# Gate weights, zeroing, denominators and expert stages moved in a fused attention and mixture-of-experts kernel

## What is computed

```
a   = attn(cond(x))             # cond: shared gated FFN and one of 3 typed gated FFNs, mixed by a gate
x   = x + a                     # attn: 16 heads of 16, causal, softmax, output projection
z   = cond2(x)                  # three shared FFNs and two of four typed ones, mixed by a gate
x   = x + ffn(z)                # router of three layers, top 2 of 8 experts, capacity 10 per sequence
```

## Time and profile before

| | |
|---|---|
| median of three runs | 2598.01 us (2594.25 to 2600.58) |
| the profiled execution | 2599.39 us, of which the span of the trace is 2597.7 us |
| PE busy | 2396.5 us, 92% of the span |
| PE weight loads | 1567.3 us, 60% |
| DVE busy | 1206.0 us, 46% |
| ACT busy | 1105.8 us, 43% |
| POOL busy | 124.6 us, 5% |
| chain that ended last | PE 79%, DVE 7%, ACT 6%, issue 3%, DMA 2% |

### The profile page before, as it was taken

One profiled execution on the slowest core, in us unless ns is written; L12 is line 12 of the kernel. 1 busy time (PEld: TensorE's weight loads), 2 busy tenths in 40 slices (PEclk: granted clock), 3 DMA queues, 4 the chain that ended last, 5 costly groups with the idle time before them and its releaser, 6 DMA issues.

```text
span 2597.7 us, 52267 instructions
## 1 busy us (share of the span) xinstructions
PE 2396.5 (92%) x18863; PEld 1567.3 (60%) x18880; DVE 1206.0 (46%) x2299; ACT 1105.8 (43%) x2097; POOL 124.6 (5%) x146
## 2 busy tenths in 40 slices
PE   6999999977988999999999999988999997689976
PEld 2444788876777444444448888883444443566654
DVE  5553455436987442333324333334443433955542
ACT  3553454434665432333323333323433342866650
POOL 0000000004331000000000000000000000000000
PEclk9999999988999999999999999998999999599995
DMA  3330111012332320210100000012111100042315
GB/s 114 98 101 29 42 49 49 16 41 61 87 99 58 100 101 25 73 57 26 56 33 25 33 12 12 12 45 65 33 32 48 48 1 1 0 146 90 98 41 129
DMA packets 145077, 141.94 MB, mean 55 GB/s; under 512 B 74608, under 2 KB 129904, under 8 KB 138416
## 3 DMA queue, kind: packets, MB, share of 16 engines
q1 hardware_dynamic: 128720, 84.01, 10.9%
q0 software_dynamic: 6864, 47.98, 5.4%
q10 hardware_dynamic: 9360, 8.13, 1.3%
HBM read 96.04 MB, written 39.85 MB: 52 GB/s over the span
## 4 chain that ended last, share of the span: by engine, by line
PE 79%; DVE 7%; ACT 6%; issue 3%; DMA 2%; SPq 1%; POOL 1%; ACTq 0%; DVEq 0%; POOLq 0%
PE ps L628 30%; PE ps L645 23%; PE ps L876 13%; PE ps L865 3%; PE ps L990 2%; PE ps L978 2%; PE ps L710 1%; DVE arena L1750 1%; PE ps L1024 1%; PE ps L742 1%; ACT misc L1276 1%; ACT arena L1275 1%; ACT misc L1153 1%; DMA arena<-eout_d 1%; ACT arena L1152 1%
## 5 line engine op out<-in xcount | busy, mean ns | idle before, releaser
L628 PE MATMUL ps<-xh,arena 128*128 (+1 forms) x5376 | 907.4, 312 | 18.3 <-DVE xh L1403 10.4
L645 PE MATMUL ps<-misc,arena 128*128 128x256 f16 (+1 forms) x4128 | 727.4, 313 | 9.2 <-DVE misc L1471 7.4
L628 PEld LDWEIGHTS ps<-xh,arena 128*128 (+1 forms) x5376 | 527.6, 98 | 288.8 <-issue 23.9
L645 PEld LDWEIGHTS ps<-misc,arena 128*128 (+1 forms) x4128 | 403.5, 98 | 223.0 <-issue 8.6
L1475 DVE SCALAR_TENSOR_TENSOR misc<-ps,misc 128x256 f16<-128x256 f32 (+1 forms) x480 | 254.9, 531 | 541.7 <-ACT misc L1085 540.8
L1085 ACT ACTIVATE misc<-ps 128x256 f16<-128x256 f32 (+1 forms) x480 | 225.0, 469 | 552.7 <-PE ps L628 552.7
L876 PE MATMUL ps<-arena 128*128 128x512 f16 x1536 | 332.8, 379 | 0.0
L876 PEld LDWEIGHTS ps<-arena 128*128 128x128 f16 x1536 | 149.7, 98 | 179.6
L1684 DVE TENSOR_TENSOR arena<-misc,arena 128x512 f16<-128x512 f32 x128 | 88.6, 692 | 254.8 <-ACT arena L1223 254.8
L1469 DVE TENSOR_TENSOR arena<-ps,misc 128x256 f32<-128x256 f32 (+1 forms) x208 | 105.2, 506 | 145.8 <-ACT misc L1081 144.7
L1222 ACT ACTIVATE misc<-ps,bias 128x512 f32<-128x512 f32 x128 | 87.8, 686 | 188.2 <-PE ps L876 181.2
(11 more groups left out here) (228 smaller groups left out, 2015.8 us busy)
## 6 DMA issues: line engine op xcount, KB each, us to landing
wstage<-in_m_w POOLq DMA_DIRECT2D x16, 1024.0 KB, 5.2
arena<-src_d SPq DMA_DIRECT2D x64, 256.0 KB, 3.8
src_d<-misc SPq DMA_DIRECT2D x24, 512.0 KB, 3.1
wstage<-in_c_wi POOLq DMA_DIRECT2D x6, 1024.0 KB, 5.7
wstage<-in_r_w POOLq DMA_DIRECT2D x5, 1024.0 KB, 5.4
eout_d<-misc SPq DMA_DIRECT2D x80, 64.0 KB, 1.9
arena<-eout_d ACTq DMA_DIRECT2D x4, 1280.0 KB, 17.5
cexp_d<-misc SPq DMA_DIRECT2D x18, 256.0 KB, 2.5
```

What stands on the lines that cost most here:

```text
L628: last = mm(ps[:, bank, col:col + p.n], weight(off, half, g, wp, k * F + f * 128), xh[:, xp, k, ds(start, p.n)], start=(k == 0 and n == 0) ...
L645: last = mm(ps[:, 4 + 2 * half + m, 0:p.n], weight(place[0], half, 2 if p.gated else 1, wp, f * D + m * 128), hid[:, st % 4, hp, 0:p.n], s ...
```

## The change

1. SP loads c_g0 and c_g1 between `stores(cs)` and `stores(ce)`; c_g1 gets columns of its own.
2. POOL no longer zeroes; DVE does, in front of `selectors`. SP's blocks of q no longer wait for POOL's zeroing, and `y_made` counts without it.
3. In PE's attention round the denominators stand between q's projection and k's. In DVE's, `o_f` stands in front of `x1_lo`.
4. PE's expert stages are fully written out, with the first layer three stages ahead and three PSUM banks; ACT reads the same banks.
5. The weight pieces move to stages 2, 3, 5, 6 (ACT) and 4 to 7 (DVE), all in the wide half. The scaling of eb2 moves from before the experts to behind stage 3 of the first.

```diff
-        gate_w2c = misc[:, 1024:1028].rearrange("p (k j) -> p k j", k=2)
+        gate_w2c = misc[:, 5632:5636].rearrange("p (k j) -> p k j", k=2)
...
         def y_made(c):
-            return 2 + 2 * (c + 1)
+            return 2 * (c + 1)
...
-            pool.wait_ge(ce.l2, 2 * ce.iters)
-            nc.gpsimd.memset(qbd_all.bitcast(F32), 0.0).then_inc(s["y_make"], 1)
-            nc.gpsimd.memset(vbd_all.bitcast(F32), 0.0).then_inc(s["y_make"], 1)
             pool.wait_ge(s["gates"], 1)
...
             stores(cs)
-            stores(ce)
-
             sp.wait_ge(s["x_lo"], 8)
             sp.dma_start(misc[:, 4608:5632], a["c_g0"]).then_inc(s["gw_in"], 16)
-            sp.dma_start(misc[:, 1024:1028], a["c_g1"]).then_inc(s["gw_in"], 16)
+            sp.dma_start(misc[:, 5632:5636], a["c_g1"]).then_inc(s["gw_in"], 16)
+            stores(ce)
...
                 sp.wait_ge(s["qk_lo"], c * 2 + 1)
-                sp.wait_ge(s["y_make"], 2)
...
-                if 0 <= i - 1 < NA:
-                    denominators(i - 1)
                 if ahead:
                     pe.wait_ge(s["y_lo"], i + 2)
                     if i - 2 >= 0:
                         pe.wait_ge(s["norm"], 2 * (i - 1))
                     projection(i + 1, 0)
+                if 0 <= i - 1 < NA:
+                    denominators(i - 1)
+                if ahead:
                     projection(i + 1, 1)
...
-                        last = mm(ps[:, st % 2, 0:n], w16(MOE_W[par][0], wp, k * F + f * 128),
-                                  xe[:, xp, k, ds(e * PER_E + c0, n)],
+                        last = mm(ps[:, (e * 16 + st) % 3, 0:n], w16(MOE_W[e % 2][0], wp, k * F + f * 128),
+                                  xe[:, xp, k, e * PER_E + c0:e * PER_E + c0 + n],
...
-            def expert(e, par, lastone=False):
-                for st in range(16):
-                    expert_out(e, par, st)
-                    if st + 2 < 16:
-                        expert_in(e, par, st + 2)
-                    elif not lastone:
-                        expert_in(e + 1, 1 - par, st - 14)
-            for st in range(2):
-                expert_in(0, 0, st)
-            expert(0, 0)
-            expert(1, 1)
-            with pe.Fori(1, NE // 2 - 1) as half_e:
-                e = half_e * 2
-                expert(e, 0)
-                expert(e + 1, 1)
-            expert(NE - 2, 0)
-            expert(NE - 1, 1, True)
+            for g in range(3):
+                expert_in(0, g)
+            for g in range(NE * 16):
+                expert_out(*divmod(g, 16))
+                if g + 3 < NE * 16:
+                    expert_in(*divmod(g + 3, 16))
...
-                    if st in (3, 4, 11, 12) and e + 1 < NE:
-                        expert_weight_high(e, int(st >= 11), int(st in (4, 12)))
+                    if st in (2, 3, 5, 6) and e + 1 < NE:
+                        expert_weight_high(e, int(st >= 5), int(st in (3, 6)))
...
+            v.memset(qbd_all, 0.0)
+            v.memset(vbd_all, 0.0)
             selectors()
...
                 if 0 <= i < NA:
                     probs_low(i, 0)
+                if 0 <= i - 1 < NA:
+                    dve.wait_ge(s["pv_mm"], 2 * i)
+                    dve.wait_ge(s["den_out"], i)
+                    v.tensor_tensor(o_f.rearrange("p k n -> p (k n)"), ps[:, 4, :], rden, ALU.mult).then_inc(s["norm"], 1)
                 if 0 <= i - 2 < NA:
                     dve.wait_ge(s["x1_hi"], i - 1)
                     cols = ds((i - 2) * CH, CH)
                     v.scalar_tensor_tensor(xh[:, 1, :, cols], x1, SX, xh[:, 0, :, cols],
                                            ALU.mult, ALU.subtract).then_inc(s["x1_lo"], 1)
-                if 0 <= i - 1 < NA:
-                    dve.wait_ge(s["pv_mm"], 2 * i)
-                    dve.wait_ge(s["den_out"], i)
-                    v.tensor_tensor(o_f.rearrange("p k n -> p (k n)"), ps[:, 4, :], rden, ALU.mult).then_inc(s["norm"], 1)
...
-            dve.wait_ge(s["eb2_in"], 16)
-            link(v.tensor_scalar(misc[:, 4608:6656], misc[:, 4608:6656], SEO, None, ALU.mult))
+            def bias_scaled():
+                dve.wait_ge(s["eb2_in"], 16)
+                link(v.tensor_scalar(misc[:, 4608:6656], misc[:, 4608:6656], SEO, None, ALU.mult))
...
+                    if fresh and st == 3:
+                        bias_scaled()
...
-                    if st in (5, 6, 12, 13) and not lastone:
-
-                        w, h = int(st >= 12), int(st in (6, 13))
+                    if st in (4, 5, 6, 7) and not lastone:
+
+                        w, h = divmod(st - 4, 2)
```

18 lines of the change are left out of this document (8 added, 10 removed).

## The result

| | before | after |
|---|---|---|
| median of five executions | 2598.01 us | 2573.07 us |
| lowest to highest | 2594.25 to 2602.52 | 2569.20 to 2587.09 |
| profiled execution, its span | 2599.39, 2597.7 | 2570.97, 2569.1 |

The change makes the kernel 0.9911 of what it was, interval 0.9896 to 0.9927: 24.9 us by the medians, where 37.5 were forecast. The forecast was 2560.5 in a range of 2551 to 2573; the median of 2573.07 lies at the range's upper edge, just outside. Four of the five executions of after lie between 2569.20 and 2573.39 us; the fifth, at 2587.09, has no profile and stays unexplained.

What follows compares the result with a forecast made beforehand. PE, busy 92% of the span, was taken as the bound, so only its idle or half-clock time could be won: 10.5 (gate) + 8.5 (attention) + 18.5 (experts) = 37.5 us off 2599.4, median 2560.5, range 2551 to 2573.

Steps and rivals of the forecast that it cites:

- Gate weights, zeroing: Gate: weights loaded early and zeroing moved to DVE start POOL's sums sooner; 10.5 us won, bounds 7.5 and 12.
- Rival 1: Gate: DVE's zeroing shuts POOL out, so the sums begin 3 us later, total 2563.5; chance 10%.
- rival 5: Gate: it still waits, for line 1501's copy or exsh; 8 us less won, total 2568.5; chance 5%.
- Experts: Experts: longer lead and moved pieces remove stalls, and the first expert starts sooner; 18.5 us won, bounds 12 and 21.
- Rival 3: Experts: the pace stays with ACT, so they win 10.5 us instead of 18.5, total 2568.5; chance 10%.
- Attention: Attention: rounds fall from 14.68 to between 13.6 and 13.9 us over 13 rounds; 8.5 us won, bounds 3 and 14.
- Putting `o_f` in front of x1_lo takes 0.7 us: Attention, DVE's round: this move shortens the loop through denominators, exponentials and low probabilities by 0.7 us per round.
- 13.9 at most: Attention: DVE's own work per round, 14.68 less its 0.78 us wait, the upper end of the new round's length.
- I take 2 us off: Attention: allowance for late transfers of q's blocks, each that had slack before now costing 0.5 to 1 us.
- rival 2: Attention: transfer of q's blocks bounds all rounds, so attention wins 3 us instead of 8.5, total 2566; chance 10%.
- The tail: Last attention rounds: win nothing, because the loads of x behind x1_lo set the end there.
- Rival 4: Attention: every transfer misses and matmuls fall to half clock, 13 rounds lose 43 us, total 2612; chance 3%.

Runs made afterwards that it cites:

- e6: Kernel before with only DVE's `o_f` moved ahead of x1_lo, the denominators left where they were; 2596.80 us beside 2595.19.
- e8: Changed kernel with one of four transfers of q's blocks per round and POOL's low half of y cut to an eighth; 2556.04 us.
- e2: Kernel before with item 3 alone (denominators between the projections, `o_f` ahead of x1_lo); 2596.59 us beside 2597.79.
- e1: Kernel before with items 1 and 2 alone (gate weights ahead of the stores of ce, zeroing by DVE); 2588.08 us beside 2597.79.
- e3: Kernel before with items 4 and 5 alone (first layers three stages ahead, weight pieces in the wide half); 2579.03 us beside 2597.79.
- e11: Kernel before with the experts' first layers three stages ahead and three banks, pieces and bias where they were; 2587.63 us in one execution.
- e12: Kernel before with weight pieces in the wide half and the bias behind stage 3, lead still two stages; 2593.09 us in one execution.
- e16: Kernel before with one of the four transfers of q's blocks per round; 2596.49 us in one execution beside 2601.70.

## Why the prediction was right and wrong

**Gate weights, zeroing (10.5 forecast, 9 to 11 measured): right.** Weights off the path, the copy at 0.17 us, exsh as the next release, and no loss by DVE's zeroing. Rival 1 is refuted, and rival 5 did not happen: the gate's matmuls start 0.27 us behind the copy. The sum took 575.5 for the first sum, between 575.0 with part of the gate at the full clock and 576.5 without. Mostly the clock is not full, and the later figure is the right one (567.6 + 8.9 = 576.5), 1 us less won and within the bounds of 7.5 to 12.

**Experts (18.5 forecast, 19.1 measured): right**, step by step: 27.8 us each, gaps only in stages 9 to 11, the start 4.4 us sooner (4.7 forecast). Rival 3 is refuted.

**Attention (8.5 forecast, 0.3 measured): wrong**, below its lower bound of 3, and this is the miss of the whole. Two steps failed:

- "Putting `o_f` in front of x1_lo takes 0.7 us", as the prediction has it. It does, and in the same stroke puts DVE's low probabilities beside POOL's low half of y, which takes 0.6 us back (1.59 to 2.19 us; e6, and e8 in reverse). The prediction had worked out exclusion for the zeroing, from the 3.11 us copy, and did not apply it to the operation that it was moving itself. The rows shown above beside the earlier trace rows would have told it: POOL's line 390 starts 0.65 us ahead of line 1571, and 1571 takes 1.59 us there and 1.22 in the other half. DVE's "13.9 at most" so was taken as room that wasn't there.
- "I take 2 us off" for the transfers. The price was rival 2's: in 10 of 15 rounds PE waits for blocks, on average 1.7 us. The prediction counted which rounds were late before and held most of the rest to have slack; half of them had less than the microsecond or so by which PE now came sooner, since 5 late rounds became 10. It gave this rival 10%, at 3 us for the attention; it alone would have put the time at 2566.

The upper bound, 14 us for the attention, was right as a bound: with both causes out of the way the rounds win 13.1 us (e8). In the range one thing was added up wrongly: 47 us off 2598 are 2551, so the low end needs all three terms at their best, and not two of three.

**The tail** was said to win nothing; it lost 1.8 us. The loss comes with item 3: the same stretch takes 1454.37 us in e2 as in after, and 1452.4 to 1453.0 in before, e1, e3, e11 and e12. PE waited 3.35 us instead of 1.77 for DVE at the first second layer of the next FFN, and fell to half clock (granted 0.50 from 848.0 to 850.5), 0.48 us a matmul instead of 0.25. PE's timeline, before and after:

```profile
859.26 1.02 PE L645 MATMUL ps<-misc,arena 128*128 128x512 f16 x4 [1.77 <-DVE misc L1475]
```

```profile
848.17 1.44 PE L640 MATMUL ps<-misc,arena 128*128 128x512 f16 x3 [3.35 <-DVE misc L1458]
```

**Rival 4** (the clock falls when transfers miss) did not happen as a rule: with 10 late rounds the mean granted clock from 650 to 800 stayed 0.99. It happened once, behind the wait of 2.37 us (granted 0.62 from 649 to 652), and that round took 16.49 us. It also exists at another wait (e16).

**Profiled execution and median.** The forecast took both as 1.4 us apart. After's profiled execution is 2.1 us under its median, before's 1.4 over its own, so that 28.4 us between the two profiles are 24.9 between the medians.

## What to carry to other kernels

When a step is taken out from between two operations, look what runs on the other engines at the moment to which the second one moves; an operation whose two instances differ in length (1.22 and 1.59 us here) already tells of a collision. A loop without visible waits for a transfer can have less than a us of slack: read the time from issue to use for each round, not the count of late ones, and issue earlier what all else waits for (one step moved here won 6 to 8 us, by its span and its median; with the loads of x and the finished tiles it was 33). And gains of two moves need not add: three stages of lead and early pieces win 1.8 us per expert together, 0.6 and -0.4 alone.

## What the chip showed that I had not expected

- A DVE zeroing of 4096 words (3.47 us, 0.85 ns per word) beside POOL left POOL's operations at their length; a DVE operation with two SBUF inputs, started 0.05 us behind POOL's of 1.16 us, took 0.97 us longer.
- PE can start on four transfers of 64 KB in pieces of some 128 bytes 4.3 us behind their first issue at best, and in the worst rounds 6.5 to 6.9; rounds in which a 16 KB instruction fetch first shows 2 to 3 us behind the issue are nearly always late (36 of 40, and 17 of 22 in five other kernels), those in which it first shows at 3.5 us seldom (3 of 11, and 0 of 19). Which rounds these are changes between kernels with the same list for PE in attention.
- After a wait of 1.2 us and 32 matmuls of two columns the clock fell to 1.2 GHz in five rounds of one execution (e16), in two of another (e6) and in one each of e3 and e11, at 1.7 us each time (4.45 instead of 2.78 us for the projections). In the other rounds with such a wait it did not fall.
